# Three message sweeps: who copies the turned rows out of PSUM, where two block-number loads stand, and who copies the table in the expansions

## What is computed

```python
for l in range(N_LAYERS):                       # 3 rounds
    m = jnp.concatenate([x[dst], x[src], edge_features], axis=-1)
    m = _ffn(m, msg_w1[l], msg_b1[l])           # relu(layernorm(m @ w + b))
    m = _ffn(m, msg_w2[l], msg_b2[l])
    agg = jax.ops.segment_sum(m, dst, num_segments=N_NODES)
    h = jnp.concatenate([x, agg], axis=-1)
    x = x + _ffn(h, upd_w[l], upd_b[l])
```

## Time and profile before

| | us |
|---|---|
| runs of the kernel | 12735.32, 12758.33, 12758.74 |
| median | 12758.33 |
| the profiled execution | 12717.2 |
| its span, on which all rows lie | 12715.5 |
| first, second and third expansion, from their first to their last instruction | 3989 to 4277, 5566 to 5854, 7021 to 7313 |
| first, second and third sweep | 4280 to 5483, 5857 to 6937, 7317 to 8403 |

### The profile page before, as it was taken

The page is one execution under the profiler, slowest core; times in us unless marked ns, Lnnn a source line. Parts: engine busy times, 40 slices in busy tenths (PEclk is TensorE's granted clock), DMA queues, the critical chain, the costliest instruction groups (busy, mean ns, idle before and its releaser), DMA issues. The chain is left out here.

```text
span 12715.5 us, 361918 instructions
## 1 busy us (share of the span) xinstructions
PE 7999.5 (63%) x118914; PEld 6445.7 (51%) x118915; DVE 6864.9 (54%) x17994; ACT 6158.9 (48%) x15953; POOL 7585.7 (60%) x9320
## 2 busy tenths in 40 slices
PE   4444444444445777778888888867676755446666
PEld 3322232222335766667666766657555533434554
DVE  4444444444554588744676366653688872136331
ACT  0333333333553599945887278852688841014000
POOL 0555555555664577756887488850688835644551
PEclk9999999999667999989999999989999986568665
DMA  8101010011888866667554855559756667669773
GB/s 351 30 29 30 29 30 28 29 29 37 284 280 244 276 199 199 189 212 252 169 170 128 326 170 169 169 117 406 237 176 175 174 272 254 205 203 357 246 240 88
DMA packets 1254090, 2290.50 MB, mean 180 GB/s; under 512 B 293083, under 2 KB 690668, under 8 KB 1231086
## 3 DMA queue, kind: packets, MB, share of 16 engines
q1 hardware_dynamic: 913742, 1129.23, 28.5%
q0 software_dynamic: 232416, 575.55, 16.0%
q10 hardware_dynamic: 107712, 582.79, 11.2%
HBM read 1381.13 MB, written 905.59 MB: 180 GB/s over the span
## 5 line engine op out<-in xcount | busy, mean ns | idle before, releaser
L625 POOL DMA_INDIRECT by_src<-sort_rec,slots x1560 | 1529.1, 980 | 1605.7 <-DVE sort_rec L699 887.6
L1259 POOL DMA_INDIRECT NEAR<-spread_f,gather_ids_l x1368 | 1326.3, 969 | 355.0 <-issue 256.5
L1334 ACT ACTIVATE z_l<-z_l,stat_l 128x64 f32<-128x64 f32 x5472 | 1437.0, 335 | 0.0
L611 ACT ACTIVATE junk<-bank,minus_one 128x384 bf16<-128x384 f32 (+1 forms) x784 | 496.9, 634 | 1284.1 <-remote 806.3
L737 PE MATMUL bank<-hots 128*49 128x49 bf16 x1568 | 147.6, 225 | 1249.5 <-ACT hots_t L594 1106.8
L745 PE MATMUL bank<-hots_t 104*128 104x128 bf16 (+3 forms) x1568 | 610.4, 464 | 432.6 <-ACT junk L611 324.4
L1401 PE MATMUL bank<-NEARB,hot_t_l 128*128 x16416 | 738.1, 196 | 207.9 <-issue 165.1
L1268 POOL TENSOR_TENSOR rest_l<-m_l 128x512 f32<-128x512 f32 x684 | 716.1, 1047 | 183.6 <-DVE m_l L1322 143.1
L1401 PEld LDWEIGHTS bank<-NEARB,hot_t_l 128*128 128x128 bf16 x16416 | 642.6, 99 | 354.6 <-issue 316.7
L1434 PE MATMUL bank<-wm_diag,zr_t_l 128*128 128x128 f32 x5472 | 807.0, 291 | 0.2 <-issue 0.2
L737 PEld LDWEIGHTS bank<-hots 128*49 128x49 bf16 x1568 | 100.6, 136 | 1317.4 <-issue 1182.3
(11 more groups left out here) (380 smaller groups left out, 26912.1 us busy)
## 6 DMA issues: line engine op xcount, KB each, us to landing
spread_f<-unit_rows_a ACTq DMA_DIRECT2D x342, 512.0 KB, 6.0
hot_t_l<-dst_hots_t SPq DMA_DIRECT2D x456, 256.0 KB
NEAR<-dst_hots SPq DMA_DIRECT2D x456, 256.0 KB
unit_hot_a<-src_hots_t SPq DMA_DIRECT2D x342, 256.0 KB, 4.2
spread<-sum_unit_rows ACTq DMA_DIRECT2D x114, 768.0 KB
spread<-last_unit_rows ACTq DMA_DIRECT2D x114, 768.0 KB
dst_hots<-NEAR SPq DMA_DIRECT2D x228, 256.0 KB
dst_hots_t<-hot_t_l SPq DMA_DIRECT2D x228, 256.0 KB
```

Of the source, the lines that this page charges most:

```text
L611: act.activation(junk[:, 0:(t + 1) * P], compared(t), ACT.Relu, bias=minus_one[:], accum_out=rank[h % 2][:, 4 * u + t:4 * u + t + 1]).then ...
L625: pool.indirect_dma_start(out=by_src, out_offset=bass.IndirectOffsetOnAxis(ap=slots[h][:, j:j + 1], axis=0), in_=rec[h][:, j, :], in_offse ...
L1259: pool.indirect_dma_start(out=far_in[h % WA][:, g * GT:(g + 1) * GT, :].rearrange("p j f -> p (j f)"), out_offset=None, in_=spread_f, in_o ...
L1334: last = act.activation(z[h % WA][:, t, :], z[h % WA][:, t, :], ACT.Relu, scale=stat[h % WA][:, 2, t:t + 1])
```

## The change

1. **Who copies the turned rows.** In sweeps 2 and 3 the copy of part 6 (`BR` to `zr_t`, 512 columns) goes from ACT to DVE. In the first sweep the four transposes write to two banks, two each; DVE copies the 256 columns of one and ACT those of the other. The ACT copy keeps its place at the end of ACT's tick. The DVE copy stands second in DVE's tick, behind part 5 and ahead of the two sums.
2. **Part 10 on DVE.** The adding to `ACC`, which stood in that second place, goes to the end of DVE's tick, with its load of window numbers.
3. **PE's load of window numbers** goes from between the transposes and L1401 to the head of the tick, ahead of the transposes' waits.
4. **Expansions.** Of the four copies of table windows POOL keeps two, DVE takes two, with a load of window numbers of its own, at the head of its tick. PE waits for both engines.

```diff
@@ spread_edges, PE
-                            pe.wait_ge(s["near"], UG * n)
+                            pe.wait_ge(s["near"], UG // 2 * n)
+                            pe.wait_ge(s["near_v"], UG // 2 * n)
@@ spread_edges, POOL
-                            w = window_ids(mybir.EngineType.Pool, 1, UG * st, UG)
+                            w = window_ids(mybir.EngineType.Pool, 1, UG * st, UG // 2)
                             at_least(pool, s["expanded"], 4 * (n - WU))
-                            for g in range(UG):
+                            for g in range(UG // 2):
@@ spread_edges, DVE, at the head of the tick
+                        if p := part(0):
+                            h, st, n, nth = p
+                            w = window_ids(mybir.EngineType.DVE, 1, UG * st + UG // 2, UG // 2)
+                            at_least(dve, s["expanded"], 4 * (n - WU))
+                            for g in range(UG // 2):
+                                dve.tensor_copy(near_of[h][:, UG // 2 + g, :, :], NEARB[:, bass.ds(w[g], 1), :, D:2 * D]
+                                                .rearrange("p a q f -> p (a q) f")).then_inc(s["near_v"], 1)
@@ mpnn_pass, banks
-            BO, BH, BR, BV, BA = bank_bf, banks[0], banks[1], banks[2:4], banks[4:6]
+            BO, BH, BV, BA = bank_bf, banks[0], banks[2:4], banks[4:6]
+            TV = GT // 2 if first else GT
+            BR = [(banks[1], q) if q < TV else (banks[6], q - TV) for q in range(GT)]
@@ mpnn_pass, DVE, between parts 5 and 4 (part 10 moves unchanged to the end of the tick)
-                        if p := part(10):
...
+                        if p := part(6):
+                            h, st, n, nth = p
+                            dve.wait_ge(s["relu_turned"], n)
+                            at_least(dve, s["v_ps"], n - 2)
+                            dve.tensor_copy(zr_t[h % 2][:, 0:TV, :].rearrange("p q n -> p (q n)"),
+                                            banks[1][:, 0:TV * P]).then_inc(s["relu_t"], 1)
@@ mpnn_pass, ACT, end of the tick
-                        if p := part(6):
+                        if first and (p := part(6)):
                             h, st, n, nth = p
                             act.wait_ge(s["relu_turned"], n)
                             at_least(act, s["v_ps"], n - 2)
-                            act.activation(flat(zr_t[h % 2]), BR[:], ACT.Copy).then_inc(s["relu_t"], 1)
+                            act.activation(zr_t[h % 2][:, TV:, :].rearrange("p q n -> p (q n)"), banks[6][:, 0:(GT - TV) * P],
+                                           ACT.Copy).then_inc(s["relu_t_act"], 1)
@@ mpnn_pass, PE, head of the tick
+                        if p := part(3):
+                            w = window_ids(mybir.EngineType.PE, 0, 2 * p[1], 2)
                         if p := part(6):
                             h, st, n, nth = p
                             pe.wait_ge(s["relu"], n)
                             at_least(pe, s["relu_t"], n - 1)
+                            if first:
+                                at_least(pe, s["relu_t_act"], n - 1)
...
                         if p := part(3):
                             h, st, n, nth = p
-                            w = window_ids(mybir.EngineType.PE, 0, 2 * st, 2)
```

More of the change, by code:

```diff
@@ L1057, in spread_edges @@
             steps = NG // UG
-            s = {n: sem(f"{n}_a{l}") for n in ("near", "expanded", "act_out", "dve_out")}
+            s = {n: sem(f"{n}_a{l}") for n in ("near", "near_v", "expanded", "act_out", "dve_out")}
             hot_in = [sem(f"hot_in{h}_a{l}") for h in range(WU)]
@@ L1188, in mpnn_pass @@
                 "key", "hot", "turned", "hot_t", "near", "z", "square1", "sum1", "root1", "rec1", "relu", "relu_turned",
-                "relu_t", "v_ps", "square2", "sum2", "root2", "rec2", "message", "rest", "piece2", "acc_ps", "acc_first",
+                "relu_t", "relu_t_act", "v_ps", "square2", "sum2", "root2", "rec2", "message", "rest", "piece2", "acc_ps", "acc_first",
                 "acc_added", "ids")}
@@ L1282, in tick @@
                             dve.reciprocal(stat[h % WA][:, 2, :], stat[h % WA][:, 1, :]).then_inc(s["rec1"], 1)
-                        if p := part(10):
+                        if p := part(6):
                             h, st, n, nth = p
-                            w = window_ids(mybir.EngineType.DVE, 0, 2 * st, 2)
-                            dve.wait_ge(s["acc_ps"], n)
-                            for g in range(2):
-                                row = ACC[:, bass.ds(w[g], 1), :].rearrange("p a f -> p (a f)")
-                                mark = s["acc_added" if g else "acc_first"]
-                                dve.tensor_tensor(row, row, BA[h % 2][:, g * D:(g + 1) * D], ALU.add).then_inc(mark, 1)
-                                dve.wait_ge(mark, n)
+                            dve.wait_ge(s["relu_turned"], n)
+                            at_least(dve, s["v_ps"], n - 2)
+                            dve.tensor_copy(zr_t[h % 2][:, 0:TV, :].rearrange("p q n -> p (q n)"),
+                                            banks[1][:, 0:TV * P]).then_inc(s["relu_t"], 1)
                         if p := part(4):
@@ L1324, in tick @@
                                                      op0=ALU.max, op1=ALU.mult).then_inc(s["message"], 1)
+                        if p := part(10):
+                            h, st, n, nth = p
+                            w = window_ids(mybir.EngineType.DVE, 0, 2 * st, 2)
+                            dve.wait_ge(s["acc_ps"], n)
+                            for g in range(2):
+                                row = ACC[:, bass.ds(w[g], 1), :].rearrange("p a f -> p (a f)")
+                                mark = s["acc_added" if g else "acc_first"]
+                                dve.tensor_tensor(row, row, BA[h % 2][:, g * D:(g + 1) * D], ALU.add).then_inc(mark, 1)
+                                dve.wait_ge(mark, n)
                     rolling(dve, steps, WB8, 10, tick)
@@ L1386, in tick @@
                             at_least(pe, s["relu_t"], n - 1)
-                            for q in range(GT):
-                                last = pe.transpose(BR[:, q * P:(q + 1) * P],
+                            if first:
+                                at_least(pe, s["relu_t_act"], n - 1)
+                            for q, (bank, at) in enumerate(BR):
+                                last = pe.transpose(bank[:, at * P:(at + 1) * P],
                                                     z[h % WA][:, 2 * q:2 * q + 2, :].rearrange("p t f -> p (t f)"), ident[:])
@@ L1428, in tick @@
                             pe.wait_ge(s["relu_t"], n)
+                            if first:
+                                pe.wait_ge(s["relu_t_act"], n)
                             at_least(pe, s["message"], n - 2)
```

## The result

| | before | after |
|---|---|---|
| median of the runs, us | 12756.32 (12735.32 to 12758.74, 4 runs) | 12939.28 (12925.84 to 12953.49, 4 runs) |
| ratio, 95% interval | | 1.0147, 1.0130 to 1.0165 |
| span of the profiled execution | 12715.5 | 12951.8 |
| sweep 1, first to last start of the adding of the gathered rows | 1171.8 | 1384.1 |
| sweep 2 | 1051.3 | 1054.2 |

The changed kernel is slower by 183 us; 12,922 was forecast. The profiled executions lie 236 us apart: 212 of it in sweep 1, 22 ahead of the first expansion, where both kernels are the same, and +3 and -4 in sweeps 2 and 3. The pair overstates the difference: the profiled execution of the kernel before (12717.2) is shorter than any of its runs in the table, and that of the changed kernel is the longest of its four.

What follows compares the result with a forecast made beforehand. A ring through PE, ACT's square and DVE bounds sweep 1, POOL sweeps 2 and 3, DMAs the expansions. Sweep 1 +164 us, the rest nothing, on the median 12758.3: 12,922 us (chance 0.78), range 12,800 to 13,090.

Steps and rivals of the forecast that it cites:

- the new ring: Sweep 1: PE, transposes, DVE's copy, two sums and keys make a tick of 5.78 us against 4.97, 0.81 more.
- What bounds the kernel: DMAs pace the expansions, a ring through PE, ACT's square and DVE sweep 1, POOL sweeps 2 and 3 (4.63 us).
- ring of 4.97 us: Sweep 1 before the change: PE's turning to second product, ACT's square, DVE's sum, keys and one-hot matrix fill the undisturbed tick.
- The excess over the undisturbed tick: Sweep 1: mean step 0.19 us above undisturbed today; 0.10 kept, giving 5.88 us, 0.72 more a step, 164 us in all.
- rival A: Sweep 1: ACT's occupancy sets the pace, so its relief saves 0.19 us a step, -43 us, 12,715; chance 0.10.
- Rival C: Sweep 1: PE's idle second ahead of the turning is true slack and hides the 0.81 us; no difference, 12,758; chance 0.06.
- Sweeps 2 and 3, nothing: POOL's work is untouched and the other ring, 4.18 us, stays under POOL's 4.63: no change, from -3 to +45 us.
- Rival B: Sweeps 2 and 3: transposes' signal or copy 0.8 us later, ring 4.98 us overtakes POOL; 160 us more, 13,082; chance 0.06.
- PE's early load of numbers: Sweep 1: covered by the 1.16 us of L1434; otherwise the ring grows by up to 0.37 us, 84 us in all.
- The adding to `ACC` at the end of the tick: Sweep 1: with its load it costs DVE 0.62 us when DVE has time, well under the 5.78 us tick.
- Expansions, nothing: DMAs set the pace at 2.48 us a unit, DVE comes to 1.8: nothing, at worst some 10 us each.
- Signs: Profile after: sweep 1 some 165 us longer, ACT at 80%, DVE idle before its copy, PE idle 1.7 us or more.

Runs made afterwards that it cites:

- swap_half_piece: Kernel before, with PE summing messages ahead of turning the one-hot matrix (sweep 1), half of POOL's last piece on DVE (sweeps 2, 3); 11199.73 us, ratio 0.9872.
- before_again: Kernel before, word for word, run once more at the later level of whole times; 11356.89 us (one run).
- pe_kept_busy: Changed kernel plus eight unread matrix products in PE's idle time in every step of sweep 1; 11514.90 us, ratio 1.0152.
- keys_first_copy: Changed kernel; sweep 1: adding to ACC second, keys, one-hot matrix, then copy and sums; sweeps 2, 3: half of POOL's last piece on DVE; 11938.01 us, ratio 1.0526.
- copy_late: Changed kernel, with DVE's copy in the first sweep moved behind the one-hot matrix; 11385.81 us, ratio 1.0034.
- copy_tick_later: Changed kernel; first-sweep copy keeps its place on DVE but waits for transposes one tick older, made in PE's idle time; 11398.27 us, ratio 1.0045.

## Why the prediction was right, and where it was not

The forecast of the whole was 17 us off, and that is in part luck. Its mechanism, the new ring, was right and is shown. But sweep 1 was to grow by 164 us and grew by 212 in the profiled pair, and the hit comes from the median of the runs, which moved less (183 us).

- *What bounds the kernel.* Right for sweep 1: taking the sum of the messages out of the ring of 4.97 us brought 4.99 to 4.87 us a step (`swap_half_piece`), as forecast. Right for sweeps 2 and 3: work taken from POOL brought 0.3 us a step.
- *The new ring, 5.78 us.* Measured 5.70. The links through PE and DVE's two sums are as worked out to 0.02 us each; the step to the copy was taken as 0.10 and is 0.04, the low end. Three cuts and one lengthening of the ring moved the undisturbed tick the way and about as far as forecast. 0.73 us a step, 166 us in all, are this term.
- *The excess over the undisturbed tick.* This is the term that was mis-sized. I kept 0.10 of the 0.19 us of the kernel before; it is 0.40 (6.10 - 5.70). I put the 0.19 down to loop turns, POOL and the ring's own engines. More than half of it was DVE's waiting for a DMA. The changed kernel's sweep has hardly any of that; whether its longer tick hides it isn't shown, since `before_again` has none either. What grew is the half clock, which the ring brings about itself: PE's idle time ahead of the turning goes from 1.0 to 1.8 us a tick, and the granted clock from 0.99 to 0.91. With that idle time filled the clock stayed at 1.00 and the excess was gone (`pe_kept_busy`). I had this idle time in the prediction (1.7 us) and didn't ask what it does to the clock. The step, 6.10 us, lies outside the 5.7 to 6.0 that I had set as the bound for the size.
- *ACT's relief* brought nothing: rival A fell. It would have been 12,715. ACT is 18 points less busy, and the sweep is longer. The page "Perfetto Trace Analysis" of the Trainium skill, section "Identifying the Most-Contended Engine", would have had ACT relieved; here the runs decide against that rule. Rival C fell too: PE's idle second was not slack, since the undisturbed tick grew by 0.73 us.
- *Sweeps 2 and 3, nothing.* Right: +3 and -4 us, and 4 and 7 us at the other level. POOL waits for the message once in the middle of sweep 2 and five times in that of sweep 3. Rival B, a ring through ACT's scaling, the copy, the sums and ACT's roots, did not come. The ring of 5.21 us in `keys_first_copy` is another one, which needs the half piece on DVE.
- *PE's early load of numbers*, covered: the 2.74 us from L1431 to the end of L1457 and the 0.43 to the end of the transposes are as before. *The adding to `ACC` at the end of the tick*, taken as free: it isn't on the ring of the changed kernel. Once the ring is cut, one tick in eight is 5.78 us long with it and 5.5 without.
- *Expansions, nothing.* Right: 284 to 292 us in every kernel, before (286 to 291) and after (284 to 289), DMA share 1.02. DVE's copy of a window takes 0.248 us, POOL's 0.347; POOL is busy 67 instead of 128 us of 260, and it doesn't matter.
- *Signs.* The copy starts 0.04 us behind the transposes, DVE is idle 0.63 us ahead of it (about 1 forecast), the sum over the second square starts 0.97 us behind the end of the transposes (1 forecast), ACT is at 76% (80 forecast), PE is idle 1.83 us (1.7 or more), and in sweep 2 PE no longer idles ahead of the table product.

## What to carry to other kernels

A moved operation that waits for an engine closes a ring if that engine waits for anything that stands behind it in the new queue. The ring costs time when it is longer than the step: add up its links. Before moving work to an idler engine, write down what it waits for and who waits for what stands behind it. Here there were two places for it that cost far less: behind what the others need (`copy_late`), or a step later (`copy_tick_later`). Then add what the longer idle time does to TensorE's clock, and relieve the engine or ring that sets the pace: here half an instruction a step taken from POOL was worth 140 us in two sweeps, and 0.2 us a step taken from the busiest engine nothing, while a ring held the sweep.

## What the hardware showed beside that

- *TensorE's clock answers to its own waits.* At a ring of 5.70 us with 1.83 us idle ahead of the turning the granted clock was 0.91 to 0.93 in sweep 1; at one of 5.96 us it was 0.81 and the median tick 7.47 us; with useless products in the idle time it was 1.00. A longer wait on PE was thus paid twice here.
- *DVE and POOL can block each other.* Two instructions with both inputs in SBUF, DVE's L773 (0.69 us) and POOL's L1249 (1.04 us), take 1.57 and 1.04 or 0.69 and 1.59 us if they start together. The Trainium skill says so on the page "SBUF — State Buffer", section "SBUF: two separate sides": the two engines share a pair of ports, whoever comes first holds it for the whole instruction, and a DVE instruction with two SBUF inputs counts among them, against a POOL instruction that reads SBUF. The rows agree: one of the two keeps its time, and the other ends shortly before both lengths (1.73 us) have passed. That the ports are the cause is the page's statement; the runs show the collision.
- *The level differs.* The kernel before took 12,756, about 11,341 and 12,694 us at three times. Between the first two, nearly all of the difference lies outside the sweeps (960 us ahead of the first expansion), and 0.17 us a step in sweep 1 (5.16 and 4.99). The cost of the change was 183 us at the first level and 260 at the second. What sets the level stays open.
